# Attention 0's value rows shared out anew, and its row statistics moved from VectorE to ScalarE

## The reference

```
h = tok(x)
h = h + attention0(layernorm(h))   # 16 heads of 16 channels, 10 tokens
h = h + experts(layernorm(h))      # router picks 2 of 8 experts for each token
h = h + attention1(layernorm(h))   # causal
h = h + low_rank(layernorm(h))     # base matrix, shared and routed rank-16 updates
```

## Time and profile before

| | us |
|---|---|
| the profiled execution's own time | 801.32 |
| its span | 799.3 |
| PE busy | 708.0 (89%) |
| DVE busy | 514.5 (64%) |
| POOL busy | 424.9 (53%) |
| ACT busy | 378.1 (47%) |
| granted TensorE clock, mean | 0.942 |

### The profile page before, as it was taken

How to read it: one execution, slowest core, us unless ns; L and a number is a source line. 1 busy time by engine, 2 the same in 40 slices (tenths; PEclk the granted TensorE clock), 3 DMA queues, 4 the chain that set the end, 5 groups by cost and what they waited for, 6 DMA issues and landing times.

```text
span 799.3 us, 13085 instructions
## 1 busy us (share of the span) xinstructions
PE 708.0 (89%) x4247; PEld 606.5 (76%) x4247; DVE 514.5 (64%) x1230; ACT 378.1 (47%) x930; POOL 424.9 (53%) x360
## 2 busy tenths in 40 slices
PE   3879999999999999999829828999999999587797
PEld 2869998988889897654528727999999999344786
DVE  5758787878778777769989871322332223488957
ACT  4466666657666665533132323444444444056131
POOL 5765767677685771448959512333433332036640
PEclk9989999999999999999868967999999999689799
DMA  7952343333423220000020078899988982300001
GB/s 234 257 168 75 114 115 94 84 109 115 113 61 114 58 81 26 1 0 1 0 106 1 27 281 302 309 326 329 327 323 328 347 314 75 129 16 2 0 1 66
DMA packets 47065, 108.58 MB, mean 136 GB/s; under 512 B 5029, under 2 KB 24729, under 8 KB 39577
## 3 DMA queue, kind: packets, MB, share of 16 engines
q1 hardware_dynamic: 44408, 100.68, 37.7%
q0 software_dynamic: 2592, 7.10, 2.4%
HBM read 101.58 MB, written 6.17 MB: 135 GB/s over the span
## 4 chain that ended last, share of the span: by engine, by line
PE 74%; DVE 12%; DMA 4%; SPq 3%; POOL 3%; ACT 2%; issue 2%; DVEq 0%; ACTq 0%; POOLq 0%
PE banks L1708 12%; PE banks L1716 12%; PE banks L291 9%; PE banks L293 9%; PE banks L292 8%; PE banks L298 6%; PE banks L304 4%; PE banks L1316 3%; SPq L386 2%; DMA xraw<-in_x_rest 2%; PE banks L1363 1%; DVE banks L1490 1%; PE banks L1290 1%; DVE a_o L1581 1%; DVE a_prod L1203 1%
## 5 line engine op out<-in xcount | busy, mean ns | idle before, releaser
L408 POOL TENSOR_TENSOR x_lo<-xraw,x_hi 128x512 fp32r<-128x512 f32 x81 | 106.1, 1309 | 84.3 <-ACT x_hi L402 84.3
L1799 ACT ACTIVATE hid<-banks,b 128x128 f32<-128x128 f32 x216 | 79.3, 367 | 110.2 <-PE banks L1708 110.2
L291 PE MATMUL banks<-wc_hi,x_hi 128*128 128x256 f32 x324 | 97.3, 300 | 16.1 <-POOL x_hi L411 13.2
L1964 DVE TENSOR_TENSOR res<-banks,xb 128x256 f32<-128x256 f32 x27 | 11.5, 424 | 127.0 <-PE banks L1716 127.0
L293 PE MATMUL banks<-wc_hi,x_lo 128*128 128x256 f32 x324 | 92.2, 285 | 0.0
L292 PE MATMUL banks<-wc_lo,x_hi 128*128 128x256 f32 x324 | 92.1, 284 | 0.0
L291 PEld LDWEIGHTS banks<-wc_hi,x_hi 128*128 128x128 f32 x324 | 62.4, 193 | 18.5 <-issue 13.4
L442 DVE BATCH_NORM_STATS2 stats<-banks 128x6 f32<-128x256 f32 x81 | 34.6, 427 | 64.8 <-ACT pe_sb L436 64.2
L1837 POOL TENSOR_TENSOR y<-bve,mhalf 128x1 f32<-128x1 f32 x27 | 20.2, 748 | 105.2 <-DVE bve L1972 105.2
L1708 PEld LDWEIGHTS banks<-xT,w_raw 128*128 128x128 f32 x448 | 67.9, 196 | 5.8 <-ACT xT L1787 0.9
L436 ACT ACTIVATE pe_sb<-banks 128x256 f32<-128x256 f32 x81 | 31.0, 383 | 85.7 <-PE banks L429 76.9
(11 more groups left out here) (331 smaller groups left out, 1861.4 us busy)
## 6 DMA issues: line engine op xcount, KB each, us to landing
w_raw<-in_w SPq DMA_DIRECT2D x28, 1024.0 KB, 6.7
xraw<-in_x_main SPq DMA_DIRECT2D x27, 768.0 KB
w1more<-in_w SPq DMA_DIRECT2D x13, 1024.0 KB
w2more<-in_w SPq DMA_DIRECT2D x13, 1024.0 KB
xraw<-in_x_rest SPq DMA_DIRECT2D x48, 96.0 KB
xraw<-in_x_rest SPq DMA_DIRECT2D x27, 114.0 KB
yl<-y_rows SPq DMA_DIRECT2D x2, 1028.0 KB, 6.9
a_w<-in_qkv_w SPq DMA_DIRECT2D x2, 768.0 KB, 5.4
```

The lines of the kernel that those rows point to most:

```text
L291: pe.matmul(dst, a[0], b[0], start=start, stop=False)
L408: pool.tensor_tensor(x_lo[:, i % RING_X, :], xraw[:, k, 0:KF].rearrange("p c b -> p (c b)"), x_hi[:, i % RING_X, 0:KF * P], ALU.subtract). ...
L1799: act.activation(hid[:, s % 2, fc, :], bank(fc % 2, 0, P), ACT.Gelu, bias=b1[:, bass.ds(e * FC + fc, 1)]).then_inc(sem("gelu_made"), 1)
```

## The change

- `POOL_VALUES[0]` loses row 2, which DVE makes now. DVE scales the second half's weights before row 3, and centres the router there.
- `copy_h` on ACT also accumulates the row's sum (in both layers). In layer 0 ACT then makes minus the mean, and squares the row minus its mean with an accumulated sum. Neither `bn_stats` nor `bn_aggr` is left for the experts' norm.
- The experts' norm has one batch of ten tiles. DVE makes the variances in `dve_route` behind the second `route_top` and the shifts behind the third. ACT normalises all ten rows after its loop.
- One semaphore of POOL's constants is joined with another.

```diff
-        BEFORE = {"class": 0, "attention 0": 0, "experts": 1, "attention 1": NW, "low rank": 2}
+        BEFORE = {"class": 0, "attention 0": 0, "attention 1": NW, "low rank": 1}
...
-                   ("experts", 0, 4), ("experts", 4, 8), ("experts", 8, T), ("attention 1", 0, 2), ("attention 1", 2, 6), ("attention 1", 6, T),
+                   ("experts", 0, T), ("attention 1", 0, 2), ("attention 1", 2, 6), ("attention 1", 6, T),
...
-        POOL_VALUES = ((0, 2, 4, 6, 8), (0, 1, 2, 3, 4, 6, 8))
+        POOL_VALUES = ((0, 4, 6, 8), (0, 1, 2, 3, 4, 6, 8))
...
-                for part in range(3):
-                    inverse_std(pool, *batch_of("experts", part))
+                inverse_std(pool, *batch_of("experts", 0))
...
-            act.activation(h_at(t), bank(6 + t % 2), ACT.Copy).then_inc(sem("a_h_made"), 1)
+            act.activation(h_at(t), bank(6 + t % 2), ACT.Copy, accum_out=row_sum_of[:, layer, t:t + 1]).then_inc(sem("a_h_made"), 1)
+
+        def square_row(act, t):
+
+            act.wait_ge(sem("a_h_made"), t + 1)
+            act.activation(mv[1][:, t, 0:1], row_sum_of[:, 0, t:t + 1], ACT.Copy, scale=-1.0 / C).then_inc(sem("row_measured"), 1)
+            act.wait_ge(sem("row_measured"), 2 * t + 1)
+            act.activation(x2[:, t * C:(t + 1) * C], h_at(t), ACT.Square, bias=mv[1][:, t, 0:1],
+                           accum_out=mv[1][:, t, 1:2]).then_inc(sem("row_measured"), 1)
...
-                if layer == 0 and t == 7:
-                    norm_rows(act, 0)
+                if layer == 0 and t:
+                    square_row(act, t - 1)
...
             copy_h(act, layer, T - 1)
             if layer == 0:
+                square_row(act, T - 1)
                 for t in range(T - 3, T):
                     copy_hT(act, t)
...
-                if layer == 0 and t == HALF:
+                if layer == 0 and t == 3:
                     softmax_half(dve, link, 0, 1)
-                if layer == 0 and i == 1:
+                if layer == 0 and i == 2:
                     center_router(dve)
...
-                while added < t - 3:
-                    add_o(dve, layer, added)
+                while layer == 1 and added < t - 3:
+                    add_o(dve, added)
                     added += 1
...
+        def row_variances(dve):
+
+            dve.wait_ge(sem("row_measured"), 2 * T)
+            dve.tensor_scalar(veps[1][:, :], mv[1][:, :, 1], 1.0 / C, 1e-5, ALU.mult, ALU.add).then_inc(sem("var_made"), 1)
+
+        def row_shifts(dve):
+
+            n = batch_of("experts", 0)[0]
+            dve.wait_ge(sem("rstd_made"), n + 1)
+            dve.tensor_tensor(nmr[1][:, :], mv[1][:, :, 0], rstd[1][:, :], ALU.mult).then_inc(sem("nmr_made"), 1)
...
-        def norm_rows(act, group):
-            normalized_scales(act, "experts", group)
-            for t in range(*GROUPS[group]):
+        def norm_rows(act):
+            normalized_scales(act, "experts")
+            for t in range(T):
...
-            norm_rows(act, 1)
-            norm_rows(act, 2)
+            norm_rows(act)
...
-            for a, b in GROUPS[1:]:
+            for a, b in GROUPS:
                 route_top(dve, link, a, b)
+                if b == T - 2:
+                    row_variances(dve)
+            row_shifts(dve)
...
-            shift_of(dve, *batch_of("experts", 2))
```

More of the change, by code:

```diff
@@ L100, in vision_tower @@
         spare = sb("spare", [P, 2])
+        row_sum_of = sb("row_sum_of", [P, 2, T])
         rstd = [sb(f"rstd{i}", [P, T]) for i in range(3)]
@@ L1582, in dve_attention, with add_o @@
                    .then_inc(sem("a_o_made"), 1)
-                while added < t - 3:
-                    add_o(dve, layer, added)
+                while layer == 1 and added < t - 3:
+                    add_o(dve, added)
                     added += 1
[L1586 to L1598, removed]
+            if layer == 1:
+                for t in range(added, T):
+                    add_o(dve, t)
+        def row_variances(dve):
[5 more added lines that the diff above has]
+            dve.tensor_tensor(nmr[1][:, :], mv[1][:, :, 0], rstd[1][:, :], ALU.mult).then_inc(sem("nmr_made"), 1)
+        def add_o(dve, t):
+            dve.wait_ge(sem("a_h_made"), seen(1, "h_made", t + 1))
+            ends = {7: 0, T - 1: 1}
+            tile_stats(dve, "low rank", t, h_at(t))
             if t in ends:
-                add_eps(dve, following, ends[t])
-            if layer == 0 and t - 1 in ends:
-                shift_of(dve, *batch_of(following, ends[t - 1]))
+                add_eps(dve, "low rank", ends[t])
         def top_two(dve, link, x, t8, ti, tf, count):
@@ L1812, in pool_route_constants @@
             pool.memset(not_first[:, :, :], 1.0).then_inc(sem("route_fill"), 1)
-            pool.wait_ge(sem("route_fill"), 2)
+            pool.wait_ge(sem("route_fill"), 3)
             pool.affine_select(out=before[:, :], in_=before[:, :], compare_op=ALU.is_gt, fill=0.0,
@@ L2180, in _ @@
         def _(pool):
-            pool.memset(ident[:, :], 0.0).then_inc(sem("ident_zeroed"), 1)
+            pool.memset(ident[:, :], 0.0).then_inc(sem("route_fill"), 1)
             pool.memset(mhalf[:, :], -0.5).then_inc(sem("consts_made"), 1)
@@ L2184, in _ @@
             pool.memset(xraw[:, :, 4, :], 0.0).then_inc(sem("pads_zeroed"), 1)
-            pool.wait_ge(sem("ident_zeroed"), 1)
+            pool.wait_ge(sem("route_fill"), 1)
             pool.affine_select(out=ident[:, :], in_=ident[:, :], compare_op=ALU.not_equal, fill=1.0,
```

## The result

The changed kernel takes 804.83 us (median; 803.33 to 807.7) and the kernel before, on the same chip, 803.01 (800.88 to 805.03): ratio 1.0027, 95% interval 1.0015 to 1.0039. A later measurement gave 804.35 against 802.89 (1.0024, 1.0014 to 1.0034). It is slower by 1.5 to 1.8 us. The forecast was +0.6, with 0.5 for no change and 0.3 for slower: the time lies in the range, the slowdown is about three times the forecast one, and the outcome with the largest chance did not come. The profiled execution took 804.31 us, its span is 802.6.

The account below looks back on a forecast made before the run. The prediction took the router's chain up to the gather as the bound, with PE pacing attention 0's rows. Router's chain +0.3 and layer 1 +0.3 made +0.6 on the median 802.9: 803.5 us, low 800.4, high 806.0.

Parts of the forecast that it names:

- 1. DVE: Attention 0's rows: DVE gains a sixth row, loses statistics and the 3.70 us block, ends row 9 at 449.45.
- 2. POOL: Attention 0's rows: without row 2, POOL ends row 8 near 445.8, hidden with 2.7 us to spare.
- 3. PE and its clock: Attention 0's rows: PE becomes the bound, starts at 1.2 GHz, regains 2.4 at 436.3, turns row 9 at 452.7.
- 4. ACT: Row statistics on ACT: square_row 1.0 to 1.1 us, read-outs 0.1; hidden except in the tail; first eight logits 1.1 us earlier.
- 5. The serial piece: Router's chain: logits to topf takes 3.7 us instead of 2.31, with a 1.95 us POOL power; topf 0.3 us later.
- 6. What follows: After the router: weights' queue starts at 469.8, gather issued at 475.9, gamma lands with 2.5 us of cover.
- 7. Layer 1: Layer 1's copies of h accumulate without use, twice in the chain: +0.3 us (0 to +0.5).
- the clock stays at 2.4 GHz: Rival, 15%: PE's gap before row 3 doesn't lower the clock; row 9 turned 1.5 us ahead: 802.0 us.
- DVE sets the pace: Rival, 12%: PE follows DVE's rows and turns row 9 at 449.5, 3.2 us ahead: 800.3 us.
- the clock comes back late: Rival, 20%: PE's clock returns at 439.7 during row 4, 1.7 us lost: 805.2 us.
- the late constants: Rival, 7%: gamma lands beyond 484.8, after the first GELU wants it; at 5 us later, 2.5 us show: 806.
- the returned block: Rival, 6%: the 3.7 us block returns with row_variances in the serial chain, 3.5 us on top: 807.

Follow-up runs that it names:

- rows only: Kernel before with row 2 on DVE, the second softmax half before row 3 and the centring moved; statistics stay on DVE in three batches: 802.94 us.
- variances first: Changed kernel with row_variances behind the first route_top instead of the second: 802.90 us, ratio 0.9997 to the kernel before.
- the repeat: The changed kernel, unedited, measured and profiled once more beside the experiments: 804.35 us, ratio 1.0024 to the kernel before.
- no accumulator: Changed kernel with copy_h accumulating in layer 0 only, not in layer 1: 804.49 us, ratio 1.0026 to the kernel before.
- five and five: Changed kernel with POOL making rows 0, 2, 4, 6, 8 and DVE five, softmax and centring placed as before, statistics on ACT: 805.90 us, again 804.10.
- tail swapped: Changed kernel with the edits of "variances first", "project row 2 first" and "no accumulator", and ACT copying hT of row 7 before squaring row 9: 800.54 us.
- gap filled: "project row 2 first" plus eleven matmuls with unused results in PE's gap before row 3: 801.97 us, ratio 0.9995 to the kernel before.
- project row 2 first: Changed kernel with PE projecting row 2 before it turns row 3: 802.07 us, ratio 0.9990 to the kernel before.

## Why the prediction was right or wrong

**1. DVE: right.** Row 9 ends at 450.30, forecast 449.45; 0.43 of that is M, the rest a row's pitch of 5.71 us instead of 5.59. The block of 3.70 is gone. `veps` took 3.70 us and ended as POOL's product did; in "rows only" it took 0.51 and ended as POOL's sum did; with POOL idle it took 0.17. The Trainium skill, page "SBUF — State Buffer", section "SBUF: two separate sides", has a pair of ports for which VectorE and GpSimd hold an exclusive lock for a whole instruction; the first two agree with it.

**2. POOL: right.** Row 8 ends at 447.19 (forecast 445.8), PE wants it at 449.46.

**3. PE and its clock: mechanism right, row 5 forecast 0.6 us too early.** PE is the bound from row 3 on, and the clock fell at the place forecast. From M row 3 came 0.24 late. Its iteration and row 4's took 7.68 us against my 7.35. I had priced the projection of row 2 at 1.8 us; the six matmuls took 2.56 at 1.2 GHz, L1364 among them with 1.06. The price was misread: I took the 1.51 us of L1363 at 425.37 for its time at 1.2 GHz, but the window from 426 has 0.96, so the clock came back in its middle. It takes 1.91 us at 1.2 GHz and 1.03 at 2.4. The clock came back near 437.0 (half of the window 436 to 438 at each level gives its 0.75), forecast 436.3, so row 4 made up part of it. From row 5 on the working was exact: 12.7 us forecast, 12.66 measured.

**4. ACT: mean and square as forecast, the tail 0.2 us short.** A read-out adds 0.10 us behind its ACTIVATE (0.48 against 0.38 in the chain), the value taken, and h to the end of the square is 1.25 us, forecast 1.0 to 1.1, within its bounds. From row 9's turn to eight logits it is 6.33 us, forecast 6.1. No table load came for the square, and the one before Exp took 1.28 us, as before.

**The term that failed** is what these two were to give: "DVE got the first eight at 459.90 before: 1.1 us gained". From M the gain is 0.34. The 0.8 missing are 0.57 up to row 5 (0.24 that row 3 came late, 0.33 of the two slow iterations) and 0.2 of the tail, step 4.

**5. The serial piece: right.** 3.73 us against 3.7 forecast, the power 1.97 against 1.95, DVE idle 1.31. Together with the missing gain `topf` is 1.08 us late from M instead of 0.3. The edit "variances first" takes this piece away, and with it 1.45 us.

**6. What follows: the covers right, one term missing.** The weights' queue starts at 470.93 (forecast 469.8), the gather at 477.22 (475.9), each late by what `topf` is late. The first GELU waits for PE's L1721 and for no DMA: the cover of 2.5 us held.

```profile
486.49 0.37 ACT L1811 ACTIVATE hid<-banks,b 128x128 f32<-128x128 f32 x1 [1.37 <-PE banks L1721]
```

But from `topf` to this GELU it is 22.77 us, and 22.56 in the repeat, against 22.30 in the kernel before, and part of that is the gather's own time, 6.75 and 6.54 us against 6.43. The sum has nothing for it.

**7. Layer 1: the pieces right,** +0.2 in the chain for +0.3; no time of "no accumulator" shows them.

Corrected, the sum on the span is 1.08 + 0.2 + 0.47 = +1.75 by the first profile and 1.18 + 0.2 + 0.26 = +1.64 by the repeat. The times say +1.5 to +1.8, and the spans 0.2 more, since 1.75 us lie around the changed kernel's span and 1.95 around that of the kernel before. So the sum fits to 0.3 us.

One thing doesn't fit in. The two profiles differ by 3.3 us in span: 0.43 of that is M, 1.08 comes at `topf`, 0.6 from there to layer 1, and 1.2 in layer 1. Of this last 0.8 is PE's clock, which came back later in the changed kernel. Its second L1346 group there, and then that of the kernel before:

```profile
751.64 2.77 PE L1346 MATMUL banks<-ident,a_prod 128*128 128x128 f32 x12
```

```profile
749.54 1.93 PE L1346 MATMUL banks<-ident,a_prod 128*128 128x128 f32 x12
```

The group's work is the same in all thirteen profiles. It takes 2.77 us in the changed kernel, its repeat, both "five and five", "no accumulator" and "tail swapped", and 1.75 to 2.44 in the other seven; with 2.77 the rest of the kernel is 0.6 to 1.5 us longer (50.9 to 51.1 us against 49.6 to 50.3). With 0.8 us of it the sum would be too large for the times. Whether it belongs to the change or varies from run to run isn't shown: the kernel before has one profile. Differences of whole spans between single profiles mislead here, which is why the marks up to `topf` carry the argument.

Of the rivals, "the clock stays at 2.4 GHz" was worked out 1.5 us below the forecast; "gap filled" against "project row 2 first" measures it at 1.66, with row 2's projection out of the slow stretch. "DVE sets the pace", "the clock comes back late" (439.7; it was 437), the late constants and the returned block did not occur.

What stays open: why the gather takes longer, the first five-and-five timing, and what sets the moment at which the clock returns in layer 1.

## What to carry to other kernels

A statistic that nobody needs soon should be started where its engine idles, not where its result is next asked for: a wait for another engine's slow power, put into a stream ahead of a critical chain, costs all of it that no work beside it covers (here 1.4 of 1.97 us), whatever was saved elsewhere. When work moves from one engine to another, price the third one that consumes both, at the clock it will have after the new gap, every matmul of it. Filling a PE gap with idle matmuls paid here when they ended before the awaited data was there, and cancelled itself when they didn't.

## What the runs showed of the hardware

- A gap of 2.42 us on PE was followed by the fall to 1.2 GHz ("project row 2 first"), one of 1.06 us after five filling matmuls was not, and one of 2.20 us in "rows five and five" was not either.
- After the same work the clock was back at 2.4 GHz in the window from 426 in the kernel before, and part of the way already in this one of the changed kernel:

```profile
422.00:424.00 2.00, 2.00 (x14) 2.00 (x13) 2.00 (x1) 0.00 (x0) 1.92 (x2) 0.66 0.00 0
```

- ACT's accumulated sum costs a separate instruction, 0.19 us long, which delays the next by about 0.1 us; a square with it runs with no table load.
- A small `tensor_scalar` of DVE (`veps`) that started while POOL had an instruction on SBUF under way ended with that instruction: 3.70 us in the kernel before, 0.51 in "rows only", 0.17 where POOL was idle. DVE's batch statistics (0.42 us) and value rows (2.82 us) ran beside POOL's products at their usual length.
- POOL's power takes 1.97 us for ten columns of 128 partitions, on the line through the 0.70 and 1.64 of the earlier trace rows.
